# Local attention layers: where scores are issued, how weights are laid out, and which engine adds the rotation's halves

## The reference, cut to what matters

```python
        q = l2norm(q) * qs
        k = l2norm(k) * ksc
        q = q * cos * scale + rotate_half(q) * sin * scale
        k = k * cos * inv + rotate_half(k) * sin * inv
        # a window's queries see their own window and the one before
        sim = jnp.einsum('bhwie,bhwje->bhwij', bq, bk2) * QK_SCALE
        sim = jnp.where(mask, -jnp.finfo(sim.dtype).max, sim)
        attn = jax.nn.softmax(sim, -1)
        out = jnp.einsum('bhwij,bhwje->bhwie', attn, bv2)
```

## Time and profile before

| | us |
|---|---|
| median of 3 runs | 5827.2 |
| lowest, highest | 5820.96, 5835.39 |
| the profiled execution | 5824.73 |
| its span in the trace | 5822.9 |
| busy in the span: PE, DVE, ACT, POOL | 4904.4, 3918.9, 2414.7, 831.2 |
| the local stage's maxima (L1720): first, last | 636.9, 2443.9 |

### The profile page before, as it was taken

The page is one execution under the profiler, slowest core; times in us unless marked ns, Lnnn a source line. Parts: engine busy times, 40 slices in busy tenths (PEclk is TensorE's granted clock), DMA queues, the critical chain, the costliest instruction groups (busy, mean ns, idle before and its releaser), DMA issues. The chain is left out here.

```text
span 5822.9 us, 69334 instructions
## 1 busy us (share of the span) xinstructions
PE 4904.4 (84%) x21823; PEld 2404.3 (41%) x21823; DVE 3918.9 (67%) x5682; ACT 2414.7 (41%) x3376; POOL 831.2 (14%) x798
## 2 busy tenths in 40 slices
PE   6888677767677777769879999999999999999993
PEld 2333343434343443423344444444444444444441
DVE  3666564646364645536558888888888888888865
ACT  1444453535353544414414444444444444444441
POOL 0000443425252534400000000000000000000000
PEclk6877788888788887868779999999999999999996
DMA  0000000000000000000000000000000000000000
GB/s 17 3 0 0 30 12 9 12 9 1 20 1 20 1 16 4 1 10 1 1 27 2 1 2 3 3 2 1 4 2 2 3 3 3 1 4 1 1 1 8
DMA packets 18034, 35.04 MB, mean 6 GB/s; under 512 B 3418, under 2 KB 12250, under 8 KB 16746
## 3 DMA queue, kind: packets, MB, share of 16 engines
q1 hardware_dynamic: 17642, 30.22, 1.6%
HBM read 29.69 MB, written 0.52 MB: 5 GB/s over the span
## 5 line engine op out<-in xcount | busy, mean ns | idle before, releaser
L1137 DVE TENSOR_REDUCE xat_part<-xat_ring 128x1 f32<-128x512 f32 (+1 forms) x1664 | 1086.0, 667 | 267.8 <-PE xat_ring L969 249.3
L1080 ACT ACTIVATE xat_p_full<-xat_sc 128x1024 f32<-128x1024 f32 (+1 forms) x816 | 835.3, 1024 | 970.9 <-PE xat_sc L1015 967.4
L1167 DVE TENSOR_TENSOR xat_p_sum<-xat_p_sum,xat_p_full 128x1024 f32<-128x1024 f32 x768 | 935.7, 1218 | 43.2 <-ACT xat_p_full L1080 35.6
L996 PE MATMUL xat_acc<-xat_p_full,xat_v 128*64 128x512 f32 (+1 forms) x3264 | 884.3, 620 | 1.5 <-ACT xat_p_full L1080 1.4
L969 PE MATMUL xat_ring<-xat_k_hl,xat_q_hh 128*128 128x512 f32 (+1 forms) x1664 | 716.9, 446 | 57.1 <-DVE xat_k_hl L1134 18.4
L1014 PE MATMUL xat_sc<-xat_q_hh,xat_k_hl 128*128 128x512 f32 (+1 forms) x1632 | 755.2, 463 | 0.0
L1015 PE MATMUL xat_sc<-xat_q_lm,xat_k_h 128*128 128x512 f32 (+1 forms) x1632 | 651.9, 399 | 0.0
L969 PEld LDWEIGHTS xat_ring<-xat_k_hl,xat_q_hh 128*128 128x128 f32 x1664 | 313.6, 190 | 713.0 <-issue 334.9
L1419 PE MATMUL loc_pr<-loc_w_qkv,loc_xs 128*128 128x512 f32 x576 | 392.4, 818 | 101.9 <-DVE loc_cosd L1684 55.9
L1836 POOL PARTITION_ALL_REDUCE quant_top<-quant_part x5 | 1.8, 357 | 2851.8 <-DVE quant_part L1859 2851.8
L1014 PEld LDWEIGHTS xat_sc<-xat_q_hh,xat_k_hl 128*128 128x128 f32 (+1 forms) x1632 | 308.9, 189 | 140.1 <-issue 95.6
(11 more groups left out here) (391 smaller groups left out, 6864.9 us busy)
## 6 DMA issues: line engine op xcount, KB each, us to landing
loc_w_qkv<-in_L_ffn_w SPq DMA_DIRECT2D x6, 1536.0 KB, 7.8
loc_w_o<-in_L_ffn_wo SPq DMA_DIRECT2D x6, 512.0 KB, 3.3
xat_ctxT<-in_ctxT SPq DMA_DIRECT2D x12, 256.0 KB, 2.7
xat_w_qk<-in_L_xattn_wqk SPq DMA_DIRECT2D x16, 128.0 KB, 2.0
loc_w<-in_L_ffn_w SPq DMA_DIRECT2D x6, 341.0 KB, 3.2
loc_w<-in_L_ffn_w SPq DMA_DIRECT2D x6, 192.0 KB, 2.4
loc_rope<-in_rope SPq DMA_DIRECT2D x1, 1024.0 KB
xat_w_o<-in_L_xattn_wo SPq DMA_DIRECT2D x16, 64.0 KB, 1.8
```

The costliest lines, as they stand in the source:

```text
L996: last = pe.matmul(acc[h * GROUP:(h + 1) * GROUP, e, :], v[0:size, t, e * GROUP:(e + 1) * GROUP], p_full[0:size, t % 3, cols(h)], start=(t ...
L1080: act.activation(p_full[0:size, j % 3, :].rearrange("p (a b) -> p a b", a=2), sc[0:size, x:x + 2, :], ACT.Exp, scale=GROUP ** -0.5).then_i ...
L1137: ins = dve.tensor_reduce(part[:, t, c:c + 1], ring[:, b, 0:chunks[c][1]], AX.X, ALU.max)
L1167: dve.tensor_tensor(p_sum[:, e, :], first_in, p_full[:, (j - 1) % 3, :], ALU.add)\
```

## The change

Five things are changed in `local_stage`:
- TensorE issues the scores of unit x at the head of step 2x-1, where they were issued at the head of step 2x. They now stand ahead of that odd step's weight transposes and preparation.
- `probs` has 160 columns a head in one piece. One subtraction and one reduction a unit take the place of two each, and the addition of two sums goes away. GpSimd reads `probs` and writes its product to a new tile `weights_n`, in the layout that `probs` had; it waits for the transpose of the unit four before.
- The addition of the rotation's two parts goes from GpSimd to VectorE, to the head of `normalise`.
- `normalise` of q goes from p=6 to p=5, and GpSimd's sine product of q from p=3 to p=2.
- q is transposed and copied out at p=6, right after k, where it was p=7.

```diff
@@ -1292,7 +1292,8 @@
         kT = s.sb("kT", [P, 3, LPAIRS, SPAN])
-        probs = s.sb("probs", [P, 4, 4 * SPAN])
+        probs = s.sb("probs", [P, 4, 4, SPAN])
+        weights_n = s.sb("weights_n", [P, 4, 4 * SPAN])
         v_more = s.sb("v_more", [P, 3, 4, LDIM])
@@ -1356,7 +1357,7 @@
 
-            return {-4: ([("k", t)], []), -1: ([("q", t)], []), 2: ([("v", t)], []), 3: ([("x", t)], []), 6: ([], ["k"]), 7: ([], ["q"])}
+            return {-4: ([("k", t)], []), -1: ([("q", t)], []), 2: ([("v", t)], []), 3: ([("x", t)], []), 6: ([], ["k", "q"])}
 
@@ -1383,7 +1384,7 @@
             for step in range(-NP - 4, STEPS + 8):
-                if step >= 0:
+                if step >= -1:
                     units(step)
@@ -1433,8 +1434,8 @@
                 def units(step):
-                    x = step // 2
-                    if step % 2 == 0 and x < UNITS:
+                    x = (step + 1) // 2
+                    if step % 2 and x < UNITS:
                         t, u = divmod(x, UN)
@@ -1456,12 +1457,12 @@
                         for c in range(4):
-                            last = pe.transpose(tr[:, n % 2, c * P:(c + 1) * P], probs[:, x % 4, c * P:(c + 1) * P],
+                            last = pe.transpose(tr[:, n % 2, c * P:(c + 1) * P], weights_n[:, x % 4, c * P:(c + 1) * P],
                                                 g.ident[:])
...
                         pe.wait_ge(S["tr_free"], i * (TR * NTOK) + (n - 1))
-                        pe.transpose(tr[:, n % 2, 0:P], probs[:, x % 4, 4 * P:4 * SPAN], g.ident[:])\
+                        pe.transpose(tr[:, n % 2, 0:P], weights_n[:, x % 4, 4 * P:4 * SPAN], g.ident[:])\
                           .then_inc(S["tr_ps"], 1)
@@ -1533,13 +1534,6 @@
                         act.activation(ss[:], ss[:], ACT.Sqrt).then_inc(S["root_done"], 1)
-                    if p == 7:
-                        for b in range(2):
-                            x = tr_at["q", t, b]
-                            act.wait_ge(S["tr_ps"], i * (TR * NTOK) + (x + 1))
-                            act.activation(qT[:, t % 2, 4 * b:4 * b + 4, :],
-                                           tr[:, x % 2, :].rearrange("p (c q) -> p c q", q=P),
-                                           ACT.Copy).then_inc(S["tr_free"], 1)
                     if p == 3:
@@ -1558,12 +1552,19 @@
                             last.then_inc(S["tr_free"], 1)
+                    if p == 6:
+                        for b in range(2):
+                            x = tr_at["q", t, b]
+                            act.wait_ge(S["tr_ps"], i * (TR * NTOK) + (x + 1))
+                            act.activation(qT[:, t % 2, 4 * b:4 * b + 4, :],
+                                           tr[:, x % 2, :].rearrange("p (c q) -> p c q", q=P),
+                                           ACT.Copy).then_inc(S["tr_free"], 1)
 
...
                     x = step // 2
-                    if step % 2 == 0 and x < UNITS:
+                    if step % 2 == 0 and 0 <= x < UNITS:
                         act.wait_ge(S["sub_done"], i * UNITS + (x + 1))
-                        act.activation(probs[:, x % 4, :], probs[:, x % 4, :], ACT.Exp).then_inc(S["exp_done"], 1)
+                        act.activation(probs[:, x % 4, :, :], probs[:, x % 4, :, :], ACT.Exp).then_inc(S["exp_done"], 1)
                     x = (step - 3) // 2
@@ -1612,7 +1613,7 @@
                 def prepare(t, p):
-                    if p not in (0, 3):
+                    if p not in (0, 2):
                         return
@@ -1624,19 +1625,18 @@
                     last.then_inc(S["sin_done"], 1)
-                    pool.wait_ge(S["sin_done"], n)
-                    pool.wait_ge(S["cos_done"], n)
-                    pool.tensor_tensor(cosd[:, w, :], cosd[:, w, :], sind[:, w, :], ALU.add)\
-                        .then_inc(S["add_done"], 1)
 
...
                         pool.wait_ge(S["inv_done"], i * UNITS + (x + 1))
-                        for lo, width in ((0, P), (4 * P, WIN)):
-                            mine = probs[:, x % 4, lo:lo + 4 * width].rearrange("p (c k) -> p c k", c=4)
-                            last = pool.tensor_tensor(mine, mine, rinv[:, x % 4, :].unsqueeze(2)
-                                                      .to_broadcast([P, 4, width]), ALU.mult)
+                        if x >= 4:
+                            pool.wait_ge(S["tr_ps"], i * (TR * NTOK) + (tr_at["e", x - 4] + 1))
+                        for lo, first, width in ((0, 0, P), (4 * P, P, WIN)):
+                            to = weights_n[:, x % 4, lo:lo + 4 * width].rearrange("p (c k) -> p c k", c=4)
+                            last = pool.tensor_tensor(to, probs[:, x % 4, :, first:first + width],
+                                                      rinv[:, x % 4, :].unsqueeze(2).to_broadcast([P, 4, width]),
+                                                      ALU.mult)
                         last.then_inc(S["p_done"], 1)
@@ -1686,6 +1686,10 @@
                     def normalise(w):
+                        dve.wait_ge(S["sin_done"], at_n(w))
+                        dve.wait_ge(S["cos_done"], at_n(w))
+                        dve.tensor_tensor(cosd[:, w, :], cosd[:, w, :], sind[:, w, :], ALU.add)\
+                           .then_inc(S["add_done"], 1)
                         dve.wait_ge(S["add_done"], at_n(w))
@@ -1708,35 +1712,28 @@
                         normalise(1)
-                    if p == 6:
+                    if p == 5:
                         normalise(0)
...
                     x = step // 2
-                    if step % 2 == 0 and x < UNITS:
+                    if step % 2 == 0 and 0 <= x < UNITS:
                         dve.wait_ge(S["s_ps"], i * UNITS + (x + 1))
...
                         if x >= 4:
-                            dve.wait_ge(S["tr_ps"], i * (TR * NTOK) + (tr_at["e", x - 4] + 1))
-                        for lo, first, width in ((0, 0, P), (4 * P, P, WIN)):
-                            to = probs[:, x % 4, lo:lo + 4 * width].rearrange("p (b c k) -> p b c k", b=2, c=2)
-                            last = dve.tensor_tensor(to, got[:, :, :, first:first + width],
-                                                     most.unsqueeze(3).to_broadcast([P, 2, 2, width]), ALU.add)
+                            dve.wait_ge(S["p_done"], i * UNITS + (x - 3))
+                        to = probs[:, x % 4, :, :].rearrange("p (b c) k -> p b c k", b=2)
+                        last = dve.tensor_tensor(to, got, most.unsqueeze(3).to_broadcast([P, 2, 2, SPAN]), ALU.add)
                         last.then_inc(S["sub_done"], 1)
...
                         dve.wait_ge(S["exp_done"], i * UNITS + (x + 1))
-                        for lo, width, to in ((0, P, rsum), (4 * P, WIN, rinv)):
-                            last = dve.tensor_reduce(to[:, x % 4, :], probs[:, x % 4, lo:lo + 4 * width].rearrange(
-                                "p (c k) -> p c k", c=4), AX.X, ALU.add)
-                        last.then_inc(S["sum_done"], 1)
-                        dve.wait_ge(S["sum_done"], i * (2 * UNITS) + (2 * x + 1))
-                        dve.tensor_tensor(rsum[:, x % 4, :], rsum[:, x % 4, :], rinv[:, x % 4, :], ALU.add)\
+                        dve.tensor_reduce(rsum[:, x % 4, :], probs[:, x % 4, :, :], AX.X, ALU.add)\
                            .then_inc(S["sum_done"], 1)
-                        dve.wait_ge(S["sum_done"], i * (2 * UNITS) + (2 * x + 2))
+                        dve.wait_ge(S["sum_done"], i * UNITS + (x + 1))
                         dve.reciprocal(rinv[:, x % 4, :], rsum[:, x % 4, :]).then_inc(S["inv_done"], 1)
                 attention(units, prepare)
```

## The result

| | before | changed |
|---|---|---|
| median, us | 5827.7 | 5756.5 |
| lowest, highest, us | 5820.96, 5835.39 | 5748.52, 5772.24 |
| the profiled execution, us | 5824.73 | 5757.14 |

The ratio is 0.9881, with a 95% interval from 0.9856 to 0.9905: 71 us faster where 84 were forecast (5743). A second measurement of the changed kernel gave 0.9883 (0.9863 to 0.9902).

What follows compares the result with a forecast made beforehand. It took the local stage's in-order loop, where VectorE idles for TensorE's scores, as the bound. A layer gains 7 x 1.8 + 1.6 + 0.2 - 0.4 = 14.0 us, six layers 84, giving 5743 us; range 5670 to 5800.

Steps and rivals of the forecast that it cites:

- The place of the scores: Local stage: unit 2's scores go ahead of the product waiting for v; its maximum starts 12.1 us after unit 0's, was 14.7.
- X still waiting: TensorE's product at L1409 still waits for ScalarE's copy of v, some 2.0 us where 3.85 stood, scores no longer behind it.
- The block of 27.5 us: Local stage loop of 8 steps, 4 units: 27.1 us plus 0.4 for the clock, 1.8 less than now.
- its own sign for a missed wait: Unit 0 later than 6.5 us after unit 3 would mean a missed wait around the transposes of k and q.
- The port: SBUF port shared by VectorE and GpSimd: q's multiplication loses 0.9 us a block to GpSimd's weights; free-port rival 5688 us, 0.17.
- The clock over the blocks: TensorE's granted clock: costs 0.4 us a block, between 0 and 1.4, where about 1.4 now; clock-as-now rival 5785 us, 0.18.
- that sign of being wrong: Granted clock in the blocks below that of now would show the clock step wrong.
- Without such a long wait: TensorE stretch of the kernel before, 757 to 763 us: clock at 0.87 without a wait like the 3.85 us one.
- The second chain: ScalarE and TensorE, from v's copy over the k product to the next k's square and copy: only 0.9 us shorter.
- VectorE's two additions: Rotation additions moved to VectorE: 1.22 us each, some 1.2 us net work a block, bearable against 6.1 us idle.
- The order of T and O: Weight transposes directly followed by output product, which waits about 1 us: last block 4.0 us a unit, 0.4 lost a layer.
- First block and end: Each layer: unit 0's scores no longer behind the q product, 1.6 us gained; shorter sum at the end, 0.2 gained.

Runs made afterwards that it cites:

- the port's removal: Changed kernel with GpSimd's weights of unit 2 waiting until VectorE has multiplied q: 5734.2 us, ratio 0.9849.
- the useless products: Changed kernel with the additions back on GpSimd and seven matrix products of no use in TensorE's wait for v: 5673.4 us, ratio 0.9736.
- the wait of 1.0 us filled: Changed kernel with three matrix products of no use between weight transposes and output product of units 26 to 31: 5731.2 us, ratio 0.9839.
- Seven useless products: Changed kernel with seven matrix products of no use in TensorE's wait for v, from the third block on: 5809.5 us, ratio 0.9974.

## Why the prediction was right, and where it was not

**The place of the scores.** Right. Unit 2 at 12.0 us, X still waiting with nothing behind it, and 32.8 us a block, as expected before that run, when the scores go back.

**The block of 27.5 us.** Right in size (27.52 and 27.60), partly by luck: two errors of about 0.5 us cancel. VectorE's chain, counted at 27.1, is shorter. Unit 3 came at 20.1 and not 20.7, and without the wait of 0.65 us ahead of Exp the block of 27.24 would be some 26.6 (an estimate). The clock costs more than the 0.4 counted: from 26.6 to the mean of 27.5 it is 0.9, an estimate too. The prediction had named its own sign for a missed wait, unit 0 later than 6.5 us after unit 3. It came 7.1 after it (745.85 to 752.99). The missed wait is that of Exp for the square and the copy of the next k. Likewise 1.8 us for each of seven blocks hit the sum, while six gained 2.0 and the seventh 0.2. (The 217.1 us in the prediction are 217.4 by its two layers and 216.6 by all six; that moves a block by less than 0.1.)

**The port.** Right in mechanism, and the rows fit the order; the multiplication lost 0.75 us rather than 0.9. "SBUF — State Buffer" in the Trainium skill ("Who interferes with whom") agrees for two inputs in SBUF: 1.95 us against 1.23. For a single input the prediction left out the exception that the section makes for VectorE's 2-port modes, of which it says that `tensor_scalar` can enter them. VectorE's bound (L1709) is such an instruction: it took 0.72 us beside GpSimd's weights and 1.17 beside GpSimd's addition in the kernel with the additions there, and both ended when GpSimd's instruction did (737.22 after 737.19, 753.48 after 753.44). As a term of the sum the port was put on the path, where it mostly is not: with a slow k product its removal left the block at 27.1 to 27.2.

**The clock over the blocks.** It rose, from 0.86 to 0.91, so that sign of being wrong did not appear. "Without such a long wait" was right for the stretch at 0.87 of the earlier trace rows only by comparison: TensorE waits 2.42 us in it, up to 761.19, and its products are slower right behind that wait.

**The second chain.** This is the step of the sum that was wrong. The prediction left the chain over the k product 0.9 us behind at full clock. In most blocks the k product ran at the lower clock (3.68 us, 1.7 longer), and that chain came 0.65 us after VectorE's. That is why the additions on GpSimd and the port's removal hardly moved these blocks, and why the useless products shortened them once the additions were gone.

**VectorE's two additions.** Called bearable, and never set against leaving them on GpSimd. They cost 58 us, nearly as much as the change gained. By the profiles (45 us apart) the seventh block gives some 16 us, the six others 13, and the first maximum 8, and the way to the residual takes 3 back. The last block gives 14 with its higher clock, without an addition in it; why the clock is higher there was not tested.

**The order of T and O.** The mechanism was right, the term was mis-sized: 0.4 us a layer forecast, 3.3 measured. The working took full clock, and at full clock it holds: in the kernel with the additions on GpSimd such a last block takes 11.85 us against 11.55 before. In the changed kernel TensorE entered the last block at 1.2 GHz, and a unit took 6.0 us; in one layer all three did. With the wait of 1.0 us filled it was 12.9 us. So the lower clock made the most of the loss.

**First block and end.** The 1.6 us of the first block do not show in the mean (30.7 both), where single layers lie between 29.5 and 33.1. No run tells whether the clock there hides it or the step was wrong; that stays open. The end gained 2.5 us instead of 0.2: the output product ran at full clock where it had begun at 0.53, and in the first layer it took 14.0 us instead of 16.8.

## What to carry to other kernels

In a hand-written order, look for what is queued behind a wait that it does not need, and move it ahead; that alone turned 32.8 us a block into 27.5. Then follow the second-longest chain as well, at both levels of the clock, and price each moved operation against leaving it: an engine that is idle on the average was not idle where the additions landed. When a sum comes out right, compare its parts too. A transpose and the product that uses it want something between them, and the last round of a loop, which has less to put there, needs its own count.

## What was not expected of the hardware

TensorE can stay at the lower clock while it is busy most of the time. In the second layer's last block of the changed kernel it was busy 4.99 to 5.04 of 6 us, never idle for longer than 1.01, and had 0.50 in three such stretches in a row. Two of them:

```profile
1136.50:1142.50 6.00, 4.99 (x31) 3.15 (x31) 2.65 (x4) 1.66 (x4) 0.17 (x1) 0.50 0.00 1
1142.50:1148.50 6.00, 4.99 (x35) 3.15 (x31) 2.65 (x4) 1.66 (x4) 1.40 (x2) 0.50 0.00 0
```

Filling a wait does not remove a low clock for certain. Seven useless products raised it at the k product and lowered it at the next unit's scores, 53 us for the worse; the same seven in a kernel with another chain were followed by 25.7 us blocks in four layers and 27.2 in two.
